# Constant matmuls in front of waiting TensorE items, in a macaron attention kernel on one core

## What is computed

```python
x = x + 0.5 * ffn(layernorm(x))
x = x + attn(layernorm(x))
x = x + 0.5 * ffn(layernorm(x))
# ffn: x @ base_W.T + base_b + (x @ shared_A.T) @ shared_B.T + sum over the best 2 of 6 experts, weighted by a softmax of x @ router_W.T
# attn: q, k, v = x @ W.T; layernorm of q and k per head; q, k *= 256 ** -0.25; causal softmax(q k.T) v, then @ Wo.T + bo
```

## Time and profile before

| | |
|---|---|
| Time, median of 3 runs | 1195.91 us (1195.37 to 1196.37) |
| Span of the profiled execution, first to last instruction | 1192.3 us |
| TensorE busy in it | 1104.1 us, 93% |
| ScalarE, VectorE, GpSimd busy | 1014.7, 467.5, 241.6 us |
| Mean granted TensorE clock | 0.975 |

### The profile page before, as it was taken

How to read it: one execution, slowest core, us unless ns; L and a number is a source line. 1 busy time by engine, 2 the same in 40 slices (tenths; PEclk the granted TensorE clock), 3 DMA queues, 4 the chain that set the end, 5 groups by cost and what they waited for, 6 DMA issues and landing times.

```text
span 1192.3 us, 22761 instructions
## 1 busy us (share of the span) xinstructions
PE 1104.1 (93%) x8884; PEld 359.6 (30%) x8884; DVE 467.5 (39%) x1181; ACT 1014.7 (85%) x1134; POOL 241.6 (20%) x377
## 2 busy tenths in 40 slices
PE   3758999999999999999999999999999999999994
PEld 3534333332323233232332232232222222222123
DVE  5678665554544353333333323423131222021114
ACT  3216788789888998999999999999999999999980
POOL 2236533222122211212022021012110101010100
PEclk9779999999999999999999999999999999999996
DMA  5022202003000300003000022000001100000000
GB/s 145 3 63 60 59 11 81 1 28 99 1 1 19 93 17 1 1 32 92 4 1 1 1 67 60 1 1 2 1 10 48 53 1 1 10 10 1 1 19 18
DMA packets 39608, 33.37 MB, mean 28 GB/s; under 512 B 8722, under 2 KB 39432, under 8 KB 39496
## 3 DMA queue, kind: packets, MB, share of 16 engines
q1 hardware_dynamic: 37364, 31.74, 9.0%
q10 hardware_dynamic: 2132, 0.12, 0.1%
HBM read 18.73 MB, written 12.85 MB: 26 GB/s over the span
## 4 chain that ended last, share of the span: by engine, by line
PE 72%; ACT 13%; issue 6%; DVE 6%; DMA 1%; POOL 1%; SPq 0%; ACTq 0%; DVEq 0%; POOLq 0%
PE ps L1190 68%; ACT ring L776 13%; PE ps L1232 2%; PE ps L1298 1%; DMA x<-in_x 1%; DVE st L807 1%; PE ps L1252 1%; DVE area L828 1%; DVE oT L1159 0%; POOL rstd L711 0%; POOL sq L532 0%; DVE x L980 0%; DVE ss L985 0%; DVE sq L1013 0%; ACT area L765 0%
## 5 line engine op out<-in xcount | busy, mean ns | idle before, releaser
L776 ACT ACTIVATE ring<-ps 128x1024 f32<-128x1024 f32 x1056 | 982.2, 1115 | 65.5 <-PE ps L1190 63.5
L1190 PE MATMUL ps<-ring,vf 128*17 128x512 f32 (+3 forms) x4608 | 559.4, 562 | 5.0 <-DVE oT L1159 4.4
L1190 PE MATMUL ps<-queries,keys 50*128 50x512 f16 (+3 forms) x2304 | 363.2, 366 | 22.1 <-ACT ring L776 4.9
L1190 PEld LDWEIGHTS ps<-queries,keys 50*128 50x128 f16 x2304 | 92.3, 93 | 475.3 <-ACT ring L776 437.3
L724 POOL TENSOR_SCALAR_AFFINE_SELECT ring<-ring 128x256 f32<-128x256 f32 (+1 forms) x224 | 103.9, 481 | 396.5 <-ACT ring L776 392.6
L1190 PEld LDWEIGHTS ps<-ring,vf 128*17 128x17 f32 x4608 | 79.7, 95 | 174.5 <-issue 144.2
L711 POOL TENSOR_TENSOR rstd<-var,minus_half 128x4 f32<-128x4 f32 x24 | 24.4, 1017 | 235.6 <-DVE var L813 235.4
L980 DVE SCALAR_TENSOR_TENSOR x<-ps,power,x 128x512 f32<-128x512 f32 x32 | 24.0, 750 | 110.7 <-PE ps L1190 110.7
L846 DVE CAST xnT<-ps 128x512 f16<-128x512 f32 x32 | 22.1, 691 | 100.0 <-PE ps L1232 100.0
L1190 PE MATMUL ps<-baseT,xnT 128*128 128x256 f16 x384 | 55.0, 283 | 3.9 <-DVE area L848 3.8
L1232 PE MATMUL ps<-ident,area 128*128 128x128 f32 x192 | 34.2, 311 | 20.0 <-DVE area L828 20.0
(11 more groups left out here) (153 smaller groups left out, 670.5 us busy)
## 6 DMA issues: line engine op xcount, KB each, us to landing
parts_d<-split SPq DMA_DIRECT2D x32, 256.0 KB, 2.6
keys<-parts_d SPq DMA_DIRECT2D x96, 64.0 KB, 2.3
queries<-parts_d SPq DMA_DIRECT2D x192, 32.0 KB
x<-in_x SPq DMA_DIRECT2D x8, 512.0 KB, 4.2
out_x<-x SPq DMA_DIRECT2D x16, 256.0 KB, 2.2
queries<-shift_d SPq DMA_DIRECT2D x64, 4.0 KB
ring<-in_base_W SPq DMA_DIRECT2D x1, 256.0 KB, 4.9
ring<-in_Wq SPq DMA_DIRECT2D x1, 256.0 KB, 3.8
```

Of the source, the lines that this page charges most:

```text
L776: act.activation(probs[:, u % RING, :], bank(2 * (u % SLOTS), 2), ACTF.Exp, bias=0.0, scale=1.0).then_inc(exp_ok, 1)
L1190: return pe.matmul(o, lhsT, rhs, start=start, stop=stop, skip_group_check=True)
```

## The change

TensorE gets 176 matmuls more in 15 places, 132 in the prelude and 44 in the tail. Each multiplies `identh` with itself, read four times over (128 by 512), into bank 6, and nothing reads the result. They stand in TensorE's queue directly in front of an item, ahead of the item's own waits. Two waits are put in front of the whole list, for `identh` and for the zeroing of bank 6, and one in front of the first of the tail, for the last read of bank 6. No other engine's instructions change.

```diff
+WARM = {
+    ("sizes", 0): 13, ("weight", 0): 17, ("sizes", 1): 18, ("weight", 3): 3, ("turn1", (0, 0)): 24, ("turn0", (1, 0)): 4, ("turnin0", 1): 8,
+    ("outer0", (1, 0)): 13, ("turn1", (1, 0)): 28, ("qk", 4): 4,
+    ("projout", (NC - 1, 0)): 10, ("turn2", (NC - 1, 0)): 19, ("inner1", NC - 1): 4, ("turnin1", NC - 1): 6, ("outer1", (NC - 1, 0)): 5,
+}
...
+            def warm(stage, n):
+
+                for _ in range(WARM.get((stage, n), 0)):
+                    mm(bank(ACC), identh[:, :], identh[:, :].unsqueeze(1).broadcast_to([P, CH // P, P]), True, True)
+
+            pe.wait_ge(const, 4)
+            pe.wait_ge(zeroed, 1)
             for stage, n in ORDER:
+                if (stage, n) == ("projout", (NC - 1, 0)):
+                    pe.wait_ge(acc_read, NG * NC)
+                warm(stage, n)
                 front_and_heads(main, stage, n)
```

## The result

| | before | after |
|---|---|---|
| median | 1196.03 us (1195.37 to 1196.37) | 1185.17 us (1184.72 to 1185.36) |
| ratio | | 0.991, 95% interval 0.9895 to 0.9924 |
| profiled execution: span | 1192.3 us | 1182.9 us |
| mean granted TensorE clock | 0.975 | 0.998 |

The medians are of four runs each, taken together.

A forecast was written before the change was run, and what follows sets the result against it. TensorE's loop was taken as fixed, prologue and tail as waiting and then at half clock. Prologue -5.3 and tail -3.25 us sum to -8.55: span 1183.7, plus 3.6 gives 1187.4 us, range 1183.0 to 1191.0.

The forecast's parts named there:

- What bounds the kernel: TensorE is busy 1017.2 of 1044.3 us in the loop, which stays; only prologue and tail, partly at half clock, shorten.
- The start: Prologue up to `weight` 0: thirteen constants behind the branch stand on the path, a loss of 4.1 us (3.4 to 4.7).
- Rival 2: Start: TensorE is free at 5 us, so the thirteen constants are hidden and 4.1 us go: 1183.3 us; chance 0.08.
- The gains behind it: Prologue after the start: constants fill waits, items run at full clock; -1.3, -0.2, -2.7, -1.65, -1.65 and -1.95 us.
- What is late next: First scores, 5.3 us earlier: queries come only 3.4 earlier, leaving 2.7 us for a landing of 2.3, just enough.
- rival 1: First scores: queries cap the prologue's gain at 3.4 us instead of 5.3: 1189.3 us; chance 0.15.
- Rival 3: Before 120 us: the prologue's net gain is given back, only the tail's stays: 1192.7 us; chance 0.10.
- The tail: After the last `values`: `projout` -1.55, `turn2` 0.6 and `inner1` -1.1 us gained at full clock, -3.25 us in all.
- rival 4: All waits: constants don't count as activity, cost 0.42 us each and overrun, about 24 us slower: 1220 us; chance 0.05.
- From the span to the time: Whole kernel: 3.6 us, by which the median 1195.9 lies above the span, added to the forecast span of 1183.7 us.
- The fall near 110 us: Attention loop: the clock is 1.00 from some 15 us to the end except near 110 us, where no constant stands.

The follow-up runs named there:

- e4: Changed kernel with all 176 constants at their places, each cut from 512 columns to 64: 1194.78 us, ratio 0.9995 to the kernel before.
- f1: The changed kernel itself measured again, as a yardstick on another chip: 1186.78 us, ratio 0.9936 to the kernel before.
- e1: Changed kernel without the thirteen constants in front of `sizes` 0: 1183.66 us, ratio 0.9912 to the kernel before.
- e3: Changed kernel with only the five tail places of constants, none in the prologue: 1190.07 us, ratio 0.9965 to the kernel before.
- f2: Changed kernel without the thirteen constants before `sizes` 0, but with eighteen ahead of the flag's load and the branch: 1184.71 us.
- f4: f2 plus five constants before chunk 1's transposes per head and ten before `values` 6: 1182.37 us, ratio 0.989 to the kernel before.
- e2: Changed kernel without constants before `sizes` 0 and with nine, not seventeen, before `weight` 0: 1183.07 us, ratio 0.9899 to the kernel before.
- f3: e2 plus five constants before chunk 1's transposes per head and ten before `values` 6: 1181.48 us, ratio 0.9892 to the kernel before.
- g2: f3 plus four constants in front of `values` 220: 1180.79 us, ratio 0.9889 to the kernel before.

## Why the prediction was right, point by point

- **What bounds the kernel.** Right: the change is worth what the prologue and the tail lose, and e4 shows that it acts through the clock. That the loop needs the same time wherever it starts holds to a few us only: from the first scores to the last `values` it is 1063.6 us before, 1062.5 after and 1065.9 in f1.
- **The start, +4.1 us.** Measured +4.2 at `weight` 0 (14.57 to 18.79). The row that decided it was the branch, against the row that put the wait down to ScalarE. e1 is the proof: without the thirteen, `sizes` 0 is back at 9.83. Rival 2 falls with that. The clock rose 4.7 us after the first constant, within the 2.7 to 5.4 taken from the bursts of the earlier trace rows. In f1, the same kernel, it rose after 2.9, and `weight` 0 was 3.2 us late: that 4.1 was met so closely is luck within the term's spread.
- **The gains behind it.** The step up to `sizes` 1 gave 1.6 us (1.3 forecast), `sizes` 1 itself 0.2 (0.2), `weight` 3 to the eviction at 37 us 2.6 (2.7), the first `squares` 1.05 at once and, two `squares` on, 1.6 in all (1.65). Summed up, the eviction of chunk 1's `outer0` stands 3.6 earlier (3.4), and the `squares` of 90.59 are 5.2 earlier (5.35).
- **What is late next, the first scores.** They came 4.6 us earlier, not 5.3, after a wait of 1.69 us for the queries. The issue that stood at 91.28 moved to 87.96, by 3.3 as forecast (3.4). What was mis-sized is the landing: I took 2.3 us, the keys' on the page of before, and it is 91.27 - 87.96 = 3.3 here, 0.6 us over the room of 2.7. Yet it is no fixed 3.3: in f1 the same issue stands at 87.31 and the scores start 2.31 us behind it, released by VectorE, so that the 2.3 would have done there. The keys before, the issue after, the first scores in f1:

```profile
keys<-parts_d SPq DMA_DIRECT2D x96, 64.0 KB, 2.3
```

```profile
87.96 0.28 SPq L606 DMA_DIRECT2D queries<-shift_d  x1
```

```profile
89.62 0.83 PE L1197 MATMUL ps<-queries,keys 50*128 50x512 f16 x8 [1.09 <-DVE xnT L855]
```

- **Rivals 1 and 3.** So rival 1 has its place, but not its price: from 120 us on the loop itself runs 5.6 to 5.8 us earlier, a little more than the 5.3. The next wait behind the first scores is for VectorE's work on chunk 1, which had the gain already: the transposes per head there start at 100.15, not 105.88. Rival 3, all of it given back, falls.
- **The tail, -3.25 us.** Measured -3.62 (e3: -3.61): `projout` 1.55 (1.55), `turn2` 0.66 (0.6), `inner1` 1.11 (1.1), and the last `outer1`, which I left out as at most 0.3, the 0.3 that are left.
- **Slower (rival 4).** It wanted constants that don't raise the clock. They do, where they have 512 columns. With 64 (e4) the clock stays at half, yet such constants are short enough to cost nothing that the medians can tell.
- **From the span to the time.** This is where most of the error lies. The spans differ by 9.4 us (8.55 forecast; the loop's 0.4 and the tail's 0.4 are the rest), and I laid 3.6 us around the span, from the median of before less the profiled span. But each run on record lies 1.7 to 1.9 us above its own span (after: 1182.9 in 1184.72). The profiled execution of before, whose time is not on record, must then have been one of the kernel's shorter ones, about 1194.1 us, and I compared it with the median of longer ones. The sum gave to that median the gain that was worked out on the shorter execution, and the median gained more; what the longer executions lose beyond the profiled one no trace shows. With 1.8, the forecast would have been 1183.75 + 1.8 = 1185.6 us; 1185.17 was measured. The 2.2 us of error are these 1.8 and 0.85 of span, less 0.45 by which the median run of after has a longer span than its profiled one.
- **The fall near 110 us** came as forecast (110.1 to 113.5). The kernel before has it at 116.1 to 119.5, in the fourth slice of the page, where TensorE's busy share is 8 tenths; the text ahead of the prediction counts only three slices at the start as below 9 tenths, and as below full clock. That such falls also come, go and change their length from run to run, and that the gain moves as well (10.86 and 7.92 us in two measurements), I had not seen.

## What to carry to other kernels

Where TensorE waits in short pieces, look for half clock in the work behind the waits, not only at the waits. Matmuls of a constant that fill the wait and end before the item is released won it back here (those of 512 columns did, in the same number and places those of 64 did not). In front of an item that already waits for nothing (here, behind the branch) each of them stands on the path, and what the profile names as the releaser may long have been done. And set a span against its own execution's time, never against the median of others.

## What the hardware showed that I had not expected

- Matmuls queued ahead of a branch run while the branch takes its 4.2 us (f2: constants from 2.18 to 8.96, branch from 5.3 to 9.5).
- The clock fell after waits as short as 0.53 and 1.08 us with matmuls between them (f1, 552 us), and in another execution of the same kernel it stayed up at the same place. One such fall cost 1.5 us there and about 1.7 in f4. The Trainium skill, in "TensorE: Matmul & The Clock Gate", Part 1, has the window in which activity is judged run freely, not restart with the kernel; a fall that comes and goes at one place agrees with that, and so does the rise at 15.41, 13.0 and 13.93 us in e2, f3 and g2, which are the same up to there.
- The spread of the kernel before, 4.4 us beside g2, shrank to 0.6 where no fall was left in any run (g2). That the clock is much of it is likely and not shown: f3 has two runs at 1.000 among a spread of 2.7 us.
- The granted clock's record reads 1.00 ahead of its first change, while constants there took some 0.42 us each (the thirteen: 5.26 us in all, the last ones at full clock already).
